# Mixture of experts with three choices per token: the inner layer's weights as a moving operand, read through a register, instead of loaded tile by tile

## The chip, the cores and the metric

One core of one Trainium2 chip runs the whole program. The metric is the device time of one execution in microseconds. The kernel is a decoder of four layers with twelve sublayers; the change is inside one of them, the feed-forward sublayer of the third layer (stage 8 in the code, `mixture_top3`). The median of three runs before is 2776.63 us (2773.84 to 2779.97).

## The reference, cut to what matters

There are 8 x 256 = 2048 tokens of 256 features. The sublayer computes, for each token, a shared expert and the three most probable of fifteen experts, each weighted with its softmax probability:

```
shared = relu(xt @ sW1 + sb1) @ sW2 + sb2
probs = softmax(xt @ router_W + router_b)
top_p, top_i = top_k(probs, 3)               # E = 15, cw holds top_p at top_i
h = relu(einsum('nd,edh->neh', xt, eW1) + eb1)   # eW1: 15 x 256 x 256
ye = einsum('neh,ehd->ned', h, eW2) + eb2        # eW2: 15 x 256 x 256
x = layernorm(x + shared + einsum('ned,ne->nd', ye, cw))
```

All of it is in 32-bit floating point.

## The kernel before, in words

Each sublayer is a block in which every engine has its own instruction list; engines meet at semaphores, and a barrier stands between blocks. The weights of a sublayer are one packed array that SP (SyncE) loads into `K.weights` while the sublayer before runs; so `W["w1"]` (32 tiles of 128 x 256, two for each expert and two for the shared one) and `W["w2"]` (the same) are both on chip when stage 8 starts.

The stage then has four parts.

1. Routing. TensorE (PE), VectorE (DVE) and ScalarE (ACT) compute the probabilities, the three choices, and for each (token, choice) a slot in a list that is sorted by expert and padded to whole tiles of 128 slots. There are `TILED` = 62 tiles, each belonging to one expert; `table` holds the expert of each tile. ACT copies the tokens into three sheets (L3014, L3017), one for each choice, 258 words a row: 256 features, the weight, and the place to which the result goes. In the kernel before sheet 0 lies on top of `W["w1"]` at the start of `K.weights`, sheet 1 above the weights, sheet 2 in the work area.
2. GpSimd (POOL) scatters the sheets into the HBM array `rows_in` with 48 indirect DMAs (L2881), while PE computes the shared expert.
3. The loop over the 62 tiles, which the change rewrites. For tile j:
   - SP loads the tile's 128 rows (129 KB, `load_rows`, L2814) into one of eight buffers `xt`; from the ninth on it waits until the scatter of the tile eight before has landed (L2813). It reads the tile's expert from `table` into a register (L2833), loads this expert's part of w1, 256 KB, from HBM into one of six places in `slots_w` (L2837), and its bias, 1 KB (L2839). At j = 8, 16, 24 and 32 it also issues a quarter of the next stage's weights, 960.5 KB (`load_next`, L2822). All of these are on SP's one queue, in this order.
   - PE turns the rows (`turn_row`, two 128 x 128 transposes, L2953), DVE copies them out of PSUM (L3119).
   - PE computes the hidden values already transposed (`hidden`): w1 is the stationary operand and the turned rows of 128 tokens are the moving one, four matmuls with 128 columns.
   - ACT applies bias and relu, one 128 x 128 half at a time, as the bias is one per partition (L3030).
   - PE multiplies with w2 (`outer`): here the hidden values are stationary and w2 is the moving operand, 256 columns, at an address that a PE register holds. PE reads eight experts at a time from `table` into registers (L2988).
   - DVE scales the result with the token's weight (L3126) and POOL scatters it to `rows_back` (L2888).

   The order on PE is written out by hand: in step j it does `turn_row(j)`, `hidden(j-1)`, `outer(j-2)`. DVE does `store_row(j)`, `store_out(j-2)`.
4. When all scatters have landed, SP loads the three results of each token (L2847), PE adds them, and the layer norm follows.

A 32-bit matmul shows as two MATMUL records (x8 for the four of `hidden`, x4 for the two of `outer`), a transpose as one.

Of the kernel before, what the change touches and what calls it, by code (L numbers as in the profile page):

```python
# [21 lines left out]
ACT = mybir.ActivationFunctionType  # L22
# [21 lines left out]
def allocate_signals(sem):  # L44
# [91 lines left out]
    S.k_rounded = sem("k_rounded")  # L136
    S.gate_stored = sem("gate_stored")
    S.zeros_done = sem("zeros_done")
    S.gate_done = sem("gate_done")
    return S, [S.x_copied, S.gate_done], 93  # L140

# [84 lines left out]
def weights_are_in(engine, K, stage):  # L226
    engine.wait_ge(K.weights_loaded, 16 * (K.stages.index(stage) + 1))
# [2533 lines left out]
def mixture_top3(nc, K):  # L2761
# [4 lines left out]
    RING, ROWS, SETS, REGS = 4, 8, 6, 8  # L2766

    above = words(8)
    sheets = [K.weights[:, 0:TILES * ROW], K.weights[:, above:above + TILES * ROW],
              A(TILES * ROW)]  # L2770
    sheets = [s.rearrange("p (i c) -> p i c", i=TILES) for s in sheets]
    got = [K.weights[:, n * 2 * TOP * D:(n + 1) * 2 * TOP * D] for n in range(4)]
    slots_w = [K.weights[:, TILES * ROW + r * KT * D:TILES * ROW + (r + 1) * KT * D].rearrange("p (k c) -> p k c", k=KT)
               for r in range(SETS)]
    bias1 = A(SETS, 2)
    xt, xT, hT, y = A(ROWS, ROW), A(2, KT, P), A(2, KT, P), A(RING, D)
    hid = A(2, GROUP)
    lT = xT.rearrange("p n k t -> p (n k t)")
    tail = tail_buffers2(A)

# [12 lines left out]
    most = hot.rearrange("p c i e -> p (c i e)")[:, 0:44 * E].rearrange("p (j e) -> p j e", e=E)  # L2793

    rows_in = K.rows_in.rearrange("(n p) c -> p n c", p=P)
    parts = K.packed[8][:, 0:32 * D].rearrange("p (e c) -> p e c", c=2 * D)
    biases = K.packed[8][:, 64 * D:64 * D + 32].rearrange("p (e m) -> p e m", m=2)
    flat = "p e c i -> p (e c i)"
    half = 2 * TILES * E
# [3 lines left out]
    with turn(nc, K) as block:  # L2803
        @block.sync
        def _(sp):
            weights_are_in(sp, K, 8)
            sp.dma_start(W["b2"][E:E + 1, 0, :], W["sb2"][E:E + 1, 0, :]).then_inc(K.bias_copied, 16)
            sp.wait_ge(S.table_done, 1)
            sp.wait_ge(K.scattered_in, 16 * TOP * TILES)
            sp.wait_ge(K.rows_cleared, 96)  # L2810
            def load_rows(j):
                if j >= ROWS:
                    sp.wait_ge(K.sent[(j - ROWS) % RING], 16 * ((j - ROWS) // RING + 1))  # L2813
                sp.dma_start(xt[:, j % ROWS, :], K.rows_in[j * P:(j + 1) * P, :]).then_inc(K.row_loaded[j % ROWS], 16)  # L2814

            def load_next(n):
                at, width = PLACE[9], words(9) // CHUNKS
                done = K.weights_part
                if n == CHUNKS - 1:
                    sp.wait_ge(K.weights_part, 16 * n)  # L2820
                    done = K.weights_loaded
                sp.dma_start(K.weights[:, at + n * width:at + (n + 1) * width],  # L2822
                             K.packed[9][:, n * width:(n + 1) * width]).then_inc(done, 16)

            with sp.register("expert") as expert:
                load_rows(0)
                load_rows(1)
                for j in range(TILED):
                    if j + 2 < TILED:
                        load_rows(j + 2)  # L2830
                    if j >= 8 and j % 8 == 0 and j // 8 <= CHUNKS:
                        load_next(j // 8 - 1)
                    sp.reg_load(expert, table[0:1, j:j + 1])  # L2833
                    e = sp.snap(expert, min_val=0, max_val=E - 1)
                    if j >= SETS:
                        sp.wait_ge(S.inner_stored, j - SETS + 1)
                    sp.dma_start(slots_w[j % SETS], parts[:, bass.ds(e, 1), :].rearrange("p e (k c) -> p (e k) c", k=KT)  # L2837
                                 ).then_inc(K.expert_loaded[j % SETS], 16)
                    sp.dma_start(bias1[:, j % SETS, :], biases[:, bass.ds(e, 1), :].rearrange("p e m -> p (e m)")  # L2839
                                 ).then_inc(K.expert_loaded[j % SETS], 16)  # L2840
            for r in range(RING):
                sp.wait_ge(K.sent[r], 16 * len(range(r, TILED, RING)))
            by_token = K.rows_back.rearrange("(b i p c) d -> b p i (c d)", b=B, i=2, p=P)
            for b in range(B):
                if b >= 4:
                    sp.wait_ge(S.back_summed, b - 3)
                sp.dma_start(got[b % 4].rearrange("p (i c) -> p i c", i=2), by_token[b]  # L2847
                             ).then_inc(K.back_loaded[b % 4], 16)

        @block.gpsimd  # L2850
        def _(p):
# [12 lines left out]
            nc.gpsimd.affine_select(out=before16, in_=before16, compare_op=ALU.is_gt, fill=0.0, base=0,  # L2864
                                    pattern=[[1, P]], channel_multiplier=-1)
            nc.gpsimd.memset(keep[:, :, 0, 0:1], 0.0).then_inc(S.pool_step, 1)
            weights_are_in(p, K, 8)
            for c in range(TOP):
                ins = nc.gpsimd.iota(sheets[c][:, :, D + 1:D + 2].rearrange("p i a -> p (i a)").bitcast(U32),
                                     pattern=[[TOP * P, TILES]], base=c, channel_multiplier=TOP)  # L2870
# [23 lines left out]
        def _(pe):  # L2894
# [53 lines left out]
            def turn_row(j):  # L2948
                pe.wait_ge(K.row_loaded[j % ROWS], 16 * (j // ROWS + 1))
                if j >= 2:  # L2950
                    pe.wait_ge(S.row_stored, j - 1)
                for k in range(KT):
                    ins = nc.tensor.transpose(K.bank[j % 2][:, k * P:(k + 1) * P], xt[:, j % ROWS, k * P:(k + 1) * P],  # L2953
                                              K.ident[:])
                ins.then_inc(S.row_turned, 1)

            def hidden(j):
                pe.wait_ge(K.expert_loaded[j % SETS], 32 * (j // SETS + 1))
                pe.wait_ge(S.row_stored, j + 1)
                if j >= 2:  # L2960
                    pe.wait_ge(S.inner_stored, j - 1)
                for m in range(2):
                    ins = mm(nc, K.bank[2 + j % 2][:, m * P:(m + 1) * P],
                             [(slots_w[j % SETS][:, k, m * P:(m + 1) * P], xT[:, j % 2, k, :]) for k in range(KT)])
                ins.then_inc(S.inner_done, 1)

            def outer(j, e):
                pe.wait_ge(S.inner_stored, j + 1)
# [6 lines left out]
            pe.wait_ge(S.y_added, B)  # L2975
            pe.wait_ge(S.shareT_stored, GROUPS)
            pe.wait_ge(S.table_done, 1)
            owners = [pe.alloc_register(f"owner{n}") for n in range(REGS)]
            of = {}
            for j in range(TILED + 2):  # L2980
                if j < TILED:
                    turn_row(j)
                if 1 <= j <= TILED:
                    hidden(j - 1)
                if 2 <= j:
                    if (j - 2) % REGS == 0:
                        n = min(REGS, TILED - (j - 2))
                        pe.reg_load(owners[0:n], table[0:1, j - 2:j - 2 + n])  # L2988
                        for i in range(n):
                            of[j - 2 + i] = pe.snap(owners[i], min_val=0, max_val=E - 1)  # L2990
                    outer(j - 2, of[j - 2])
            def sum_back(b):
                pe.wait_ge(K.back_loaded[b % 4], 16 * (b // 4 + 1))
                if b >= 4:
# [14 lines left out]

        @block.scalar  # L3010
        def _(a):
            weights_are_in(a, K, 8)
            for c in (2, 0):
                nc.scalar.copy(sheets[c][:, :, 0:D], K.x_tok[:]).then_inc(S.x_copied, 1)  # L3014
            a.wait_ge(S.max_done, 1)
# [9 lines left out]
            for j in range(TILED):  # L3025
                a.wait_ge(S.inner_done, j + 1)
                if j >= 2:
                    a.wait_ge(S.out_done, j - 1)
                for m in range(2):
                    ins = nc.scalar.activation(hT[:, j % 2, m, :], K.bank[2 + j % 2][:, m * P:(m + 1) * P], ACT.Relu,  # L3030
                                               bias=bias1[:, j % SETS, m:m + 1])
                ins.then_inc(S.inner_stored, 1)
            for b in range(B):
                batch_store(nc.scalar.copy, a, K, b, 6 + b % 2)

        @block.vector
        def _(v):
# [91 lines left out]
            for j in range(TILED + 2):  # L3129
                if j < TILED:  # L3130
                    store_row(j)
                if j >= 2:
                    store_out(j - 2)

            def add_back(b):
                x2 = K.x_tok[:, 2 * b:2 * b + 2, :]
# [1654 lines left out]
```

## Time and profile before

| | us |
|---|---|
| median of three runs | 2776.63 |
| the profiled execution's own time | 2774.84 |
| its span, first to last instruction | 2773.1 |
| stage 8, first instruction | 1289.8 |
| first and last turn of a row tile in the loop | 1387.45, 1542.86 |
| PE busy over the whole span | 2315.0 (83%) |

The profile is of one execution. Times within it are microseconds from the start of the span. The granted clock is given as a share of TensorE's full 2.4 GHz; a stretch at 0.5 is at 1.2 GHz. PE's busy time is a sum over overlapping records, so in the loop the start of one group and the start of the next say more than the length of either.

### The profile page before, as it was taken

What the parts mean: (1) busy time and instruction counts of PE and PEld (TensorE: products, weight loads), DVE (VectorE), ACT (ScalarE), POOL (GpSimd) and SP (SyncE); (2) the same over time, 40 slices, a digit from 0 to 9 for tenths busy, and PEclk for the clock granted to TensorE, in tenths of its full rate; (3) what the DMA queues carried; (4) which work ended last, traced back from release to release, by engine and by line L of the source; (5) the groups of instructions that cost most, each with busy time, mean ns of one, the idle gap of its engine ahead of it and who ended that gap; (6) DMA issues with size and microseconds to landing.
All of it is one profiled execution on the core that took longest, in us unless ns stands there. A gap on an engine that the chain in (4) does not pass through costs nothing. (4 is left out here: it accounts for less than half of the span.)

```text
span 2773.1 us, 39253 instructions
## 1 busy us (share of the span) xinstructions
PE 2315.0 (83%) x13092; PEld 1663.2 (60%) x13092; DVE 1422.1 (51%) x4229; ACT 1025.0 (37%) x2591; POOL 699.1 (25%) x656
## 2 busy tenths in 40 slices
PE   7985499878869839985788789698899798899898
PEld 5763377655547518864367566465466576466576
DVE  3555022256758765547123467544677443677454
ACT  3433111145525510035022156343565432565432
POOL 1102311110024343211633200263443100433111
PEclk9987699979969859997799899899999999999899
DMA  9032211173000010030287411400000000000000
GB/s 245 1 151 81 83 50 42 46 150 13 1 6 1 5 53 1 1 126 1 92 240 209 145 36 25 152 11 31 1 1 1 1 1 1 1 1 1 20 23 20
DMA packets 121173, 143.66 MB, mean 52 GB/s; under 512 B 47507, under 2 KB 101013, under 8 KB 119184
## 3 DMA queue, kind: packets, MB, share of 16 engines
q1 hardware_dynamic: 112240, 120.16, 15.5%
q0 software_dynamic: 8736, 20.99, 2.1%
q8 instruction: 109, 1.79, 0.3%
q14 instruction: 88, 0.72, 0.1%
HBM read 96.18 MB, written 47.90 MB: 52 GB/s over the span
## 5 line engine op out<-in xcount | busy, mean ns | idle before, releaser
L249 PE MATMUL bank<-work,weights 128*128 128x256 f32 (+3 forms) x2432 | 541.3, 380 | 42.2 <-DMA work<-in_weights 21.1
L249 PEld LDWEIGHTS bank<-work,weights 128*128 128x128 f32 (+1 forms) x2432 | 415.5, 193 | 138.2 <-DMA work<-in_weights 27.8
L249 PE MATMUL bank<-weights,work 128*128 128x256 f32 (+4 forms) x1520 | 412.6, 409 | 53.1 <-POOL work L2318 35.0
L249 PEld LDWEIGHTS bank<-weights,work 128*128 128x128 f32 (+1 forms) x1520 | 278.5, 196 | 152.7 <-issue 68.3
L633 POOL TENSOR_TENSOR work<-work,minus_half 128x2 f32<-128x2 f32 x96 | 69.7, 726 | 859.0 <-DVE work L626 859.0
L249 PE MATMUL bank<-weights,x_feat 128*128 128x512 f32 (+2 forms) x576 | 211.5, 500 | 25.5 <-PEq L211 14.6
L658 ACT COPY x_feat<-bank 128x512 f32<-128x512 f32 x80 | 46.7, 584 | 343.3 <-PE bank L650 342.9
L249 PEld LDWEIGHTS bank<-weights,x_feat 128*128 128x128 f32 x576 | 106.1, 196 | 84.2 <-issue 60.1
L249 PE MATMUL bank<-x_feat,weights 128*128 128x256 f32 (+3 forms) x400 | 120.4, 479 | 35.6 <-PEq L211 31.0
L4090 ACT ACTIVATE work<-work 128x128 f32<-128x128 f32 (+1 forms) x256 | 137.0, 543 | 1.5 <-DVE work L4162 1.5
L1523 DVE TENSOR_TENSOR work<-bank,work 128x384 f32<-128x384 f32 (+1 forms) x64 | 31.4, 491 | 189.6 <-ACT work L1441 189.6
L249 PEld LDWEIGHTS bank<-x_feat,weights 128*128 128x128 f32 (+1 forms) x400 | 79.5, 217 | 65.3 <-issue 51.7
L650 PE MATMUL bank<-ident,x_tok 128*128 128x128 f32 x320 | 61.2, 325 | 46.1 <-DVE x_tok L641 44.0
L249 PE MATMUL bank<-work 128*128 128x256 f32 (+3 forms) x326 | 72.9, 362 | 31.1 <-ACT work L2692 7.6
L3030 ACT ACTIVATE work<-bank,work 128x128 f32<-128x128 f32 x124 | 38.7, 363 | 141.9 <-PE bank L249 129.5
L4482 DVE SCALAR_TENSOR_TENSOR work<-bank,weights,work 128x256 f32<-128x256 f32 x96 | 45.5, 481 | 87.4 <-ACT work L4420 86.3
L3905 POOL TENSOR_TENSOR work<-work,minus_half 128x8 f32<-128x8 f32 x32 | 52.4, 1636 | 144.4 <-DVE work L4206 144.4
L1341 POOL DMA_INDIRECT rows_back<-work x40 | 38.8, 971 | 195.3 <-DVE work L1531 195.3
L2888 POOL DMA_INDIRECT rows_back<-work x62 | 60.2, 972 | 106.3 <-DVE work L3126 83.4
L4420 ACT ACTIVATE work<-bank,weights 128x256 f32<-128x256 f32 x80 | 37.9, 474 | 128.8 <-PE bank L249 128.7
L4154 DVE CUSTOM_DVE_ANT_0 work<-bank,work 128x128 f32<-128x128 f32 (+1 forms) x256 | 75.7, 352 | 16.9 <-PE bank L3953 16.9
L3126 DVE TENSOR_SCALAR work<-bank,work 128x256 f32<-128x256 f32 x62 | 30.0, 484 | 105.5 <-PE bank L249 75.8
(461 smaller groups left out, 4651.3 us busy)
## 6 DMA issues: line engine op xcount, KB each, us to landing
weights<-in_weights SPq DMA_DIRECT2D x62, 256.0 KB
weights<-in_weights SPq DMA_DIRECT2D x1, 12296.0 KB
weights<-in_weights SPq DMA_DIRECT2D x1, 9360.0 KB
weights<-in_weights SPq DMA_DIRECT2D x1, 8488.0 KB
work<-rows_in SPq DMA_DIRECT2D x62, 129.0 KB
rows_in<-ident SPq DMA_DIRECT2D x2, 3968.0 KB, 36.7
weights<-rows_back SPq DMA_DIRECT2D x8, 768.0 KB, 4.5
work<-rows_in SPq DMA_DIRECT2D x8, 645.0 KB, 4.2
```

The source lines that it names most:

```text
L249: ins = nc.tensor.matmul(out, lhsT, rhs, start=(i == 0), stop=(i == len(pairs) - 1))
L633: nc.gpsimd.tensor_tensor(t.rstd[:, n, :], t.rstd[:, n, :], K.minus_half[:, 0:2], ALU.pow).then_inc(K.S.rstd_done, 1)
L650: ins = nc.tensor.transpose(K.bank[bank][:, (2 * k + i) * P:(2 * k + i + 1) * P], K.x_tok[:, 2 * b + i, k * P:(k + 1) * P], K.ident[:])
L658: copy(K.x_feat[:, :, b * L:(b + 1) * L], K.bank[bank][:, :].rearrange("p (k t) -> p k t", k=KT)).then_inc(K.S.xT_stored, 1)
L1341: nc.gpsimd.indirect_dma_start(K.rows_back, bass.IndirectOffsetOnAxis(ap=to, axis=0), y[:, r, :], None, bounds_check=TOP * T - 1, oob_is_e ...
L2888: nc.gpsimd.indirect_dma_start(K.rows_back, bass.IndirectOffsetOnAxis(ap=to, axis=0), y[:, r, :], None, bounds_check=TOP * T - 1, oob_is_e ...
L3030: ins = nc.scalar.activation(hT[:, j % 2, m, :], K.bank[2 + j % 2][:, m * P:(m + 1) * P], ACT.Relu, bias=bias1[:, j % SETS, m:m + 1])
L3905: nc.gpsimd.tensor_tensor(rk, norm[:, 1, :], K.minus_half[:, 0:H], ALU.pow).then_inc(S.rk_done, 1)
L4090: ins = nc.scalar.activation(probs[:, u % 3, s, at:at + width], probs[:, u % 3, s, at:at + width], ACT.Exp, bias=bias[:, u % 2, i, s:s + 1 ...
L4154: ins = nc.vector.tensor_tensor_reduce(probs[:, u % 3, s, at:at + width], K.bank[SM[s]][:, at:at + width], seen[:, at:at + width], 1.0, -3 ...
L4420: nc.scalar.activation(gelu[:, n % 2, :], K.bank[n % RING][:, L:2 * L], ACT.Gelu, bias=W["b1"][:, layer, HT + f:HT + f + 1]).then_inc(S.ge ...
L4482: nc.vector.scalar_tensor_tensor(out=hid[rows, b % 2, f, :], in0=K.bank[n % RING][rows, 0:L], scalar=W["b1"][rows, layer, f:f + 1], in1=ge ...
```

## The change

- The load of each tile's part of w1 (L2837) and its six places go. `inner` takes w1 where it lies, as the moving operand at an address in a PE register, with the turned rows as the stationary operand: two matmuls with 256 columns in place of four with 128. Its result has the tokens in the partitions, so it must be turned: ACT copies it to `mid` (128 x 256), PE turns it with two transposes into bank 6 or 7 (`turn_mid`), and ACT applies bias and relu to that as before (`rectify`).
- The order on PE in step t becomes `turn_row(t)`, `inner(t-1)`, `turn_mid(t-2)`, `outer(t-3)`: one step more from the rows to the result. ACT does `store_mid(t-1)`, `rectify(t-2)`; DVE `store_row(t)`, `store_out(t-3)`. The eight experts are read into registers before `inner` instead of before `outer`, into two sets of registers in turn.
- Sheets 0 and 1 now both lie above the weights, so that w1 stays whole. POOL no longer waits for the weights, and ACT waits for them after the first two sheets instead of before.
- Two semaphores are added to the range that each barrier clears (93 to 95).

```
-    slots_w = [K.weights[:, TILES * ROW + r * KT * D:...]...]
+    mid = hid[:, 0, :].rearrange("p (n d) -> p n d", n=2)
...                                                        # SP
-                    sp.dma_start(slots_w[j % SETS], parts[:, bass.ds(e, 1), :]...).then_inc(K.expert_loaded[j % SETS], 16)
                     sp.dma_start(bias1[:, j % SETS, :], biases[:, bass.ds(e, 1), :]...).then_inc(K.expert_loaded[j % SETS], 16)
...                                                        # PE
-            def hidden(j):
-                pe.wait_ge(K.expert_loaded[j % SETS], 32 * (j // SETS + 1))
+            def inner(j, e):
                 pe.wait_ge(S.row_stored, j + 1)
+                if j >= 2:
+                    pe.wait_ge(S.mid_stored, j - 1)
+                mm(nc, K.bank[2 + j % 2][:, 0:D],
+                   [(xT[:, j % 2, k, :], W["w1"][:, bass.ds(2 * e + k, 1), :].rearrange("p o c -> p (o c)"))
+                    for k in range(KT)]).then_inc(S.inner_done, 1)
+            def turn_mid(j):
+                pe.wait_ge(S.mid_stored, j + 1)
                 if j >= 2:
                     pe.wait_ge(S.inner_stored, j - 1)
                 for m in range(2):
-                    ins = mm(nc, K.bank[2 + j % 2][:, m * P:(m + 1) * P],
-                             [(slots_w[j % SETS][:, k, m * P:(m + 1) * P], xT[:, j % 2, k, :]) for k in range(KT)])
-                ins.then_inc(S.inner_done, 1)
+                    ins = nc.tensor.transpose(K.bank[6 + j % 2][:, m * P:(m + 1) * P], mid[:, j % 2, m * P:(m + 1) * P], K.ident[:])
+                ins.then_inc(S.mid_turned, 1)
...
+            for t in range(TILED + 3):
+                if t < TILED:
+                    turn_row(t)
+                if t % REGS == 1 and t <= TILED:           # eight experts into owners[at:at + n]
+                    pe.reg_load(owners[at:at + n], table[0:1, t - 1:t - 1 + n])
+                if 1 <= t <= TILED:
+                    inner(t - 1, of[t - 1])
+                if 2 <= t <= TILED + 1:
+                    turn_mid(t - 2)
+                if 3 <= t:
+                    outer(t - 3, of[t - 3])
...                                                        # ACT
+            def store_mid(j):
                 a.wait_ge(S.inner_done, j + 1)
+                if j >= 2:
+                    a.wait_ge(S.mid_turned, j - 1)
+                nc.scalar.copy(mid[:, j % 2, :], K.bank[2 + j % 2][:, 0:D]).then_inc(S.mid_stored, 1)
+            def rectify(j):
+                a.wait_ge(S.mid_turned, j + 1)
+                a.wait_ge(K.expert_loaded[j % SETS], 16 * (j // SETS + 1))
```

## Rows read from the trace of the kernel before

**Rows 1.** Windows, the loop as one: length, busy time (instructions) of each engine, granted clock, DMA share, GB/s
```profile
1387.00:1548.00 161.00, 137.80 (x868) 120.35 (x868) 50.64 (x124) 38.73 (x124) 58.29 (x60) 0.94 0.75 216
```

**Rows 2.** Waits in the loop, 1387 to 1548: us in total, times, longest
```profile
PE bank L249 <- DMA work<-in_weights: 21.1, 15, 3.8
SPq L2814 <- DMA rows_back<-work: 20.8, 21, 2.7
```

**Rows 3.** Timeline of one undisturbed step: start, us, instructions [idle before]
```profile
1444.57 1.06 PE L249 MATMUL bank<-work,weights 128*128 128x128 f32 x8
1445.46 1.03 PE L249 MATMUL bank<-weights,work 128*128 x4
1445.66 0.62 ACT L3030 ACTIVATE work<-bank,work 128x128 f32<-128x128 f32 x2 [1.35 <-PE bank L249]
1446.33 0.38 PE L2953 MATMUL bank<-ident,work 128*128 128x128 f32 x2
1446.53 0.48 DVE L3126 TENSOR_SCALAR work<-bank,work 128x256 f32<-128x256 f32 x1 [1.16 <-issue]
1446.55 1.06 PE L249 MATMUL bank<-work,weights 128*128 128x128 f32 x8
1447.79 0.97 POOL L2888 DMA_INDIRECT rows_back<-work  x1 [1.01 <-issue]
```

**Rows 4.** Timeline at the loop's start and end
```profile
1385.28 1.29 SPq L2814 DMA_DIRECT2D work<-rows_in  x3
1387.45 1.09 PE L2953 MATMUL bank<-ident,work 128*128 128x128 f32 x4 [14.72 <-DMA work<-rows_in]
1390.19 2.07 PE L249 MATMUL bank<-work,weights 128*128 128x128 f32 x8 [1.65 <-DMA work<-in_weights]
1394.51 0.38 PE L2953 MATMUL bank<-ident,work 128*128 128x128 f32 x2
...
1542.86 0.38 PE L2953 MATMUL bank<-ident,work 128*128 128x128 f32 x2
1547.87 0.48 DVE L3126 TENSOR_SCALAR work<-bank,work 128x256 f32<-128x256 f32 x1 [0.60 <-PE bank L249]
```

**Rows 5.** Timeline around the first `load_next`, and after the third
```profile
1400.50 0.97 POOL L2888 DMA_INDIRECT rows_back<-work  x1 [1.00 <-issue]
1404.21 0.33 SPq L2814 DMA_DIRECT2D work<-rows_in  x1
1404.45 0.97 POOL L2888 DMA_INDIRECT rows_back<-work  x1 [1.01 <-issue]
1404.59 0.42 SPq L2822 DMA_DIRECT2D weights<-in_weights  x1
1410.47 0.33 SPq L2814 DMA_DIRECT2D work<-rows_in  x1
1411.14 1.16 PE L249 MATMUL bank<-work,weights 128*128 128x128 f32 x8 [2.76 <-DMA work<-in_weights]
...
1452.45 2.08 PE L249 MATMUL bank<-work,weights 128*128 128x128 f32 x8 [3.77 <-DMA work<-in_weights]
```

**Rows 6.** Sources: the 128 x 256 copy of ACT elsewhere, and PE's register loads (ns min/median/max)
```profile
L3368 ACT COPY work<-bank x16: 372/372/405, 1627.4 to 1767.3; 128x256 f32<-128x256 f32 x16
L2988 PEldq TENSOR_LOAD <-work x8: 588/602/1021, 1392.1 to 1536.4; - x8
```

**Rows 7.** Timeline of a step with a register load
```profile
1516.93 1.16 PE L249 MATMUL bank<-work,weights 128*128 128x128 f32 x8 [0.51 <-DMA work<-in_weights]
1518.46 1.13 PE L249 MATMUL bank<-weights,work 128*128 x4 [0.37 <-issue]
```

**Rows 8.** Stage 9, 1650 to 1700 as a window, and transposes among PE's groups, 1650 to 1750
```profile
1650.00:1700.00 50.00, 48.67 (x338) 34.07 (x337) 35.39 (x84) 31.76 (x113) 3.31 (x5) 1.00 0.12 24
L3267 PE MATMUL bank<-ident,work 128*128 128x128 f32 x163 | 21.9, 277 | 0.0
```

**Rows 9.** Timeline at the start of stage 8
```profile
1289.82 3.62 ACT L3014 COPY work<-x_tok 128x4096 f32<-128x4096 f32 x1 [1.24 <-PEq L211]
```

More of the change, by code:

```diff
@@ L138, in allocate_signals @@
     S.zeros_done = sem("zeros_done")
+    S.mid_stored = sem("mid_stored")
+    S.mid_turned = sem("mid_turned")
     S.gate_done = sem("gate_done")
-    return S, [S.x_copied, S.gate_done], 93
+    return S, [S.x_copied, S.gate_done], 95
 SPEC = {
@@ L2768, in mixture_top3 @@
     above = words(8)
-    sheets = [K.weights[:, 0:TILES * ROW], K.weights[:, above:above + TILES * ROW],
+    sheets = [K.weights[:, above:above + TILES * ROW], K.weights[:, above + TILES * ROW:above + 2 * TILES * ROW],
               A(TILES * ROW)]
@@ L2772, in mixture_top3 @@
     got = [K.weights[:, n * 2 * TOP * D:(n + 1) * 2 * TOP * D] for n in range(4)]
-    slots_w = [K.weights[:, TILES * ROW + r * KT * D:TILES * ROW + (r + 1) * KT * D].rearrange("p (k c) -> p k c", k=KT)
-               for r in range(SETS)]
     bias1 = A(SETS, 2)
@@ L2795, in mixture_top3 @@
     rows_in = K.rows_in.rearrange("(n p) c -> p n c", p=P)
-    parts = K.packed[8][:, 0:32 * D].rearrange("p (e c) -> p e c", c=2 * D)
     biases = K.packed[8][:, 64 * D:64 * D + 32].rearrange("p (e m) -> p e m", m=2)
@@ L2836, in _ @@
                         sp.wait_ge(S.inner_stored, j - SETS + 1)
-                    sp.dma_start(slots_w[j % SETS], parts[:, bass.ds(e, 1), :].rearrange("p e (k c) -> p (e k) c", k=KT)
-                                 ).then_inc(K.expert_loaded[j % SETS], 16)
                     sp.dma_start(bias1[:, j % SETS, :], biases[:, bass.ds(e, 1), :].rearrange("p e m -> p (e m)")
@@ L2866, in _ @@
             nc.gpsimd.memset(keep[:, :, 0, 0:1], 0.0).then_inc(S.pool_step, 1)
-            weights_are_in(p, K, 8)
             for c in range(TOP):
@@ L2962, in hidden @@
                 for m in range(2):
-                    ins = mm(nc, K.bank[2 + j % 2][:, m * P:(m + 1) * P],
-                             [(slots_w[j % SETS][:, k, m * P:(m + 1) * P], xT[:, j % 2, k, :]) for k in range(KT)])
-                ins.then_inc(S.inner_done, 1)
+                    ins = nc.tensor.transpose(K.bank[6 + j % 2][:, m * P:(m + 1) * P], mid[:, j % 2, m * P:(m + 1) * P],
+                                              K.ident[:])
+                ins.then_inc(S.mid_turned, 1)
             def outer(j, e):
@@ L2977, in _ @@
             pe.wait_ge(S.table_done, 1)
-            owners = [pe.alloc_register(f"owner{n}") for n in range(REGS)]
+            owners = [pe.alloc_register(f"owner{n}") for n in range(2 * REGS)]
             of = {}
[L2980 to L2991, printed above, removed]
+            for t in range(TILED + 3):
+                if t < TILED:
+                    turn_row(t)
+                if t % REGS == 1 and t <= TILED:
+                    n = min(REGS, TILED - (t - 1))
+                    at = (t - 1) // REGS % 2 * REGS
+                    pe.reg_load(owners[at:at + n], table[0:1, t - 1:t - 1 + n])
+                    for i in range(n):
+                        of[t - 1 + i] = pe.snap(owners[at + i], min_val=0, max_val=E - 1)
+                if 1 <= t <= TILED:
[4 more added lines that the diff above has]
+                    outer(t - 3, of[t - 3])
             def sum_back(b):
@@ L3011, in _ @@
         def _(a):
-            weights_are_in(a, K, 8)
             for c in (2, 0):
                 nc.scalar.copy(sheets[c][:, :, 0:D], K.x_tok[:]).then_inc(S.x_copied, 1)
+            weights_are_in(a, K, 8)
             a.wait_ge(S.max_done, 1)
@@ L3024, in _ @@
                                          bias=W["b1"][:, 0, 2 * E + m:2 * E + m + 1]).then_inc(S.hid_stored, 1)
-            for j in range(TILED):
+            def store_mid(j):
                 a.wait_ge(S.inner_done, j + 1)
+                if j >= 2:
[4 more added lines that the diff above has]
+                a.wait_ge(K.expert_loaded[j % SETS], 16 * (j // SETS + 1))
                 if j >= 2:
@@ L3029, in _ @@
                 for m in range(2):
-                    ins = nc.scalar.activation(hT[:, j % 2, m, :], K.bank[2 + j % 2][:, m * P:(m + 1) * P], ACT.Relu,
+                    ins = nc.scalar.activation(hT[:, j % 2, m, :], K.bank[6 + j % 2][:, m * P:(m + 1) * P], ACT.Relu,
                                                bias=bias1[:, j % SETS, m:m + 1])
                 ins.then_inc(S.inner_stored, 1)
+            for t in range(1, TILED + 2):
+                if t <= TILED:
+                    store_mid(t - 1)
+                if t >= 2:
+                    rectify(t - 2)
             for b in range(B):
@@ L3127, in store_out @@
                                         ALU.mult).then_inc(S.out_stored, 1)
[L3129 to L3133, printed above, removed]
+            for t in range(TILED + 3):
+                if t < TILED:
+                    store_row(t)
+                if t >= 3:
+                    store_out(t - 3)
             def add_back(b):
```

## The prediction

> **What bounds the kernel now.** I read the windows first, then the waits of the loop, then its timeline, then the start of the stage. The windows show the loop over the 62 row tiles as 161 us with PE busy for 138 of them, the DMA engines for three quarters of the time and a granted clock of 0.94 [rows 1]. The waits say what PE lacks: the expert's w1 from HBM, 15 times and 21.1 us in all, up to 3.8 us at once [rows 2]. In the timeline the turns of tile 0 start at 1387.45 and those of tile 61 at 1542.86 [rows 4]: 155.4 us for 61 steps, 2.55 a step. An undisturbed step is shorter [rows 3]: `hidden` 0.89 (1444.57 to 1445.46), `outer` 0.87 (to 1446.33), the two turns 0.22 (to 1446.55), 1.98 together, and PE is never idle in it. 61 x 1.98 is 120.8, so 34.6 us of the loop is not PE's own work at full clock. It is 21.1 of waits on w1 and, beyond that, half clock: 0.06 of 161 us of clock missing means 19 us at half clock, of which about half, 9.7, is lost. The rest, 4, is smaller gaps. The half clock is partly a child of the waits: after the idle 3.77 us at 1452.45 the eight matmuls of `hidden` take 2.08 instead of 1.06 [rows 5].
>
> Two things make w1 late. The four `load_next` transfers go ahead of it on SP's queue: after the first (1404.59) PE idles 2.76, after the third 3.77 [rows 5]; there are four of them. And between them it is a ring: SP issues the rows of tile j+8, and behind them w1 of tile j+6, only when the scatter of tile j has landed, and SP is seen waiting for that 21 times [rows 2].
>
> **The change, part by part.** The profiled execution took 2774.84, 1.8 below the median of the runs; I work on its trace and add the difference at the end.
>
> *PE's work in a step.* `hidden` (0.89) becomes `inner`, the same shape as `outer`: two matmuls of 256 columns, 0.87. Two more transposes cost 0.22. The step is 0.22 + 0.87 + 0.22 + 0.87 = 2.18, 0.20 more than now. Over 61 steps that is 12.2 us of loss.
>
> *The load of w1.* With it go all waits on it, and 62 x 256 KB, 16 MB of some 35. What is next on PE? Each of its waits reaches back to work of a step before. ACT had 0.62 of work in a step [rows 3] and gets a copy of 128 x 256 at 0.37 [rows 6], about 1.0 of 2.18; `rectify` ends some 1.2 before `outer` wants it, and the copy to `mid` 1.5 before `turn_mid` does. DVE (0.48 and a row copy) and POOL (0.97 a scatter) have as much to do as now.
>
> *The ring, one step deeper.* `outer` of tile j now ends four steps after `turn_row(j)`, not three. From PE's step end at 1446.33 DVE ends at 1447.01 and POOL starts the scatter at 1447.79 [rows 3], 1.5 later. From scatter to the release of SP I take 3.7 (1400.50 to 1404.21, [rows 5]; this includes SP's own delay), from the issue of rows to the first turn 2.2 (1385.28 to 1387.45, [rows 4]). That makes 7.4. The next turn in the same buffer has 4 x 2.18 = 8.7 of time. So the rows come 1.3 us early and PE sets the pace. The bias, issued behind the rows, is wanted only by `rectify`, more than two steps later than the rows.
>
> *The four `load_next`.* A scatter issued just before the first (1404.45) released SP only at 1410.47, 6.0 instead of 3.7 [rows 5]. 2.3 more, less 1.3 of slack, is 1.0 of idle for each, 4 in all, where now they cost some 13 and two falls of the clock. Bounds: nothing, when the lighter traffic lets them pass sooner; 3.4 each, 13.6, when the rows end up as late as w1 did. I take 1.0, nearest to the scatter's row, and no clock loss from it, since even after the idle 2.76 the eight matmuls take 1.16, the time at full clock [rows 5].
>
> *The start.* Tile 0 still turns at 1387.45, as that hangs on the rows. Now `hidden(0)` waits for w1 until 1390.19 and the turns of tile 3 start at 1394.51 [rows 4]. Without the wait `inner(0)` starts once DVE has copied tile 0, about 1388.65; at half clock its 1.73, turn and `inner(1)` of 0.44 + 1.73 and `turn_mid(0)` of 0.44 give tile 3 at 1393.0. Then 58 steps of 2.18 are 126.4, and with 4 for `load_next` and 0.5 for chance tile 61 turns at 1523.9.
>
> *The end.* Now the last result is at 1547.87 + 0.48, 5.5 after the turn of tile 61 [rows 4]. The new tail has the rest of step 61, then 0.87 + 0.22 + 0.87, then 0.22 + 0.87, then 0.87, about 0.35 for ACT before the last `outer` and 0.6 for DVE: 7.1. So the last result comes at 1531.0 instead of 1548.35: 17.4 us earlier. Behind it nothing changes: scatter, loads, sum and norm move forward as they are.
>
> *Register work.* The address of `inner` costs register instructions on PE's sequencer, and the load of eight registers takes 0.59 to 1.02 [rows 6]. I cost both at nothing: `outer` has the same addresses and streams at 0.87 with no gap. Exposed, a register load costs this: at 1516.93 `hidden` began after a wait and `outer` followed 1.53 later instead of 0.89, 0.64 lost [rows 7]. The upper bound is that in every step, 39 us; below nothing there is no reason to go. I take zero: in the undisturbed steps PE's stream has no gap, and after the change the waits that let PE's sequencer fall behind are gone.
>
> *The rest.* ACT's copies started right at the start of the stage (1289.82, idle only for the barrier), so the weights' wait cost nothing and moving it gains nothing [rows 9]; the same for POOL, whose first work stood before its own wait. The sheets are the same size in other places. Relu, copy and exponential follow one another in this stage with no table load of ACT. Two more semaphores in a range that one instruction clears: nothing, at most 0.1 a barrier.
>
> **Two rules weighed.** Four transposes now stand in a step, 0.44 of 2.18, a fifth of PE's time. In stage 9 there are 163 transposes of one line alone in 100 us, at 0.11 each 18 us of PE's stream, at a granted clock of 1.00 [rows 8]. The Trainium skill, page "TensorE: Matmul & The Clock Gate" (Part 4: PE-mode transpose), says that transposes do not count as a busy PE for the clock. By that rule the loop could fall to half clock; the trace shows the share that the change reaches without it.
>
> The rows of tile 0 took 2.2 with little traffic about [rows 4], and I use the same in the loop. The Trainium skill, page "DMA: Bandwidth & Descriptors" (Latency and other measured facts), holds that a lighter load on HBM lowers the fixed cost of a transfer. By it the slack of the ring would grow and `load_next` cost nothing, 4 us more gained; by the row, nothing.
>
> **Rivals.**
> - *`load_next` keeps its price.* The rows queue behind it as w1 did. For: rows and w1 share SP's queue. Against: the rows are issued two tiles ahead and w1 was not. 3.4 each instead of 1.0, and two half-clock stretches of 7 us, 7 lost: 16.6 less gain, 2776. A middle way, 2.5 each, gives 2765.
> - *No stall at all.* 4.5 more gained, 2755.
> - *PE's sequencer becomes the bound* (slower). `inner` needs a register address, one more semaphore wait and a dependence on ACT in each step; if it cannot run ahead, each step shows a gap before `inner`. For: the 0.64 of [rows 7]. Against: `outer` does it in every step unseen. It decides from 17.4 / 61 = 0.29 a step; at 0.5 a step, 30 us, the time is 2790.
> - *Half clock in the loop* (slower), if transposes do not count: 61 more steps of 2.18, 133 less 17: 2892.
> - *Later clock.* The stretches at half clock after the loop may shift by one or two of them: 5 us either way.
>
> **How the numbers follow.** The forecast is 2774.84 - 17.4 = 2757.4 by the profiled execution, 2759.2 against the median. Chances: forecast with `load_next` at 0 to 2 us each, 0.70; price kept wholly or mostly, 0.16; the sequencer, 0.07; half clock, 0.02; something that cancels to no change, 0.05. The range from 2750 (no stall, and a favourable clock) to 2769 (3 us for each `load_next`, or an unfavourable clock) leaves 0.2 out. A measurement of this kernel can tell 0.2%, 5.5 us, from no change: faster 0.87, within 0.05, slower 0.08.
>
> **What would show it.** In the profile after: no wait on `in_weights` on PE in the loop; steps of 2.18 with `inner` at 0.87 and four transposes of 0.11; the granted clock of the loop at 0.97 or more; the loop's turns spanning about 136 us; PE waiting about four times for `rows_in`, a microsecond each; DMA near 130 GB/s. Steps of 2.4 and more without a DMA wait would prove me wrong on the sequencer or ACT; waits of 3 us and more on `rows_in`, on the ring.

## The result, and the profile after

The changed kernel takes 2755.43 us (median of five runs, 2751.02 to 2756.06), the kernel before 2774.82 in the same five rounds (2769.97 to 2779.97): ratio 0.9925, 95% interval 0.9909 to 0.9941, which is a gain of 21 us, or between 16 and 25. Forecast were 2759.2 and a gain of 17.4. One execution of e7 (2799.47 us) and one of the kernel before beside e9 to e12 (2989.53) ran at a lower granted clock and are in no median or ratio below.

First the loop as a window (the length, busy time of PE, its weight loads, DVE, ACT, POOL, then granted clock, DMA share and GB/s), against [rows 1]:

```profile
1385.00:1525.00 140.00, 136.32 (x736) 115.66 (x737) 49.77 (x121) 55.40 (x184) 57.00 (x59) 0.98 0.47 132
```

Both windows stop just short of the last result, so the loop's length is read further down, from the first turn to the last result. The granted clock is 0.98 where it was 0.94, and the DMA traffic 132 GB/s where it was 216. ACT works 55 us where it worked 39, and is still far from full. The waits of the changed loop after its start (us in total, times, longest), against [rows 2]:

```profile
PE bank L2950 <- DMA work<-rows_in: 3.0, 3, 1.3
PEld bank L2967 <- issue: 0.2, 1, 0.2
```

PE waited 21.1 us for w1; now it waits 3.0 for rows, three times. After the loop's start PE waits nowhere in front of `inner`. The timeline of a step, against [rows 3] (L2950 is `turn_row`, L2967 `turn_mid`, L3036 the copy to `mid`, L3044 `rectify`; the first line of L251 is `inner`, the second `outer`):

```profile
1393.35 0.38 PE L2950 MATMUL bank<-ident,work 128*128 128x128 f32 x2
1393.57 1.03 PE L251 MATMUL bank<-weights,work 128*128 x4
1394.43 0.38 PE L2967 MATMUL bank<-ident,work 128*128 128x128 f32 x2
1394.63 0.37 ACT L3036 COPY work<-bank 128x256 f32<-128x256 f32 x1 [1.27 <-PE bank L251]
1394.65 1.03 PE L251 MATMUL bank<-weights,work 128*128 x4
1394.81 0.97 POOL L2885 DMA_INDIRECT rows_back<-work  x1 [13.43 <-DVE work L3146]
1394.90 0.63 ACT L3044 ACTIVATE work<-bank,work 128x128 f32<-128x128 f32 x2
1395.52 0.38 PE L2950 MATMUL bank<-ident,work 128*128 128x128 f32 x2
```

Read PE's lines by their starts: 0.22 + 0.86 + 0.22 + 0.87 = 2.17, and the next step begins without a gap. The ends of the loop, against [rows 4]:

```profile
1385.19 1.21 PE L2950 MATMUL bank<-ident,work 128*128 128x128 f32 x4 [14.51 <-DMA work<-rows_in]
1386.89 2.07 PE L251 MATMUL bank<-weights,work 128*128 x4 [0.49 <-DVE work L3139]
...
1520.72 0.38 PE L2950 MATMUL bank<-ident,work 128*128 128x128 f32 x2
...
1527.18 0.48 DVE L3146 TENSOR_SCALAR work<-bank,work 128x256 f32<-128x256 f32 x1 [0.55 <-PE bank L251]
```

From the first turn to the last result it is 142.5 us (1385.19 to 1527.66) where it was 160.9: 18.4 less. The whole span is 18.8 less. The remaining 0.4 is the sum of two larger differences: the loop starts 2.3 us earlier, and what follows it takes 1.9 longer. I put both down to chance, though the change also moved the sheets and two waits ahead of the loop. The start varies by itself: in the kernels below the first turn lies anywhere from 1382.5 to 1387.6, and in e11, whose work before the loop is that of the kernel before to the instruction, it lies at 1383.37 where the kernel before has 1387.45. I therefore compare the loops of the profiles by their own length, from the turn of tile 0 to that of tile 61, beside the ratios of the runs.

Around the first `load_next`, against [rows 5]:

```profile
1402.46 0.43 SPq L2822 DMA_DIRECT2D weights<-in_weights  x1
1403.48 0.97 POOL L2885 DMA_INDIRECT rows_back<-work  x1 [1.20 <-DVE work L3146]
1408.10 0.33 SPq L2814 DMA_DIRECT2D work<-rows_in  x1
1409.37 1.63 SPq L2814 DMA_DIRECT2D work<-rows_in  x1
1411.91 0.33 PE L2950 MATMUL bank<-ident,work 128*128 128x128 f32 x1 [1.06 <-DMA work<-rows_in]
```

The scatter that follows it starts at 1403.48; SP issues the rows that hang on it 4.6 later (1408.10), and PE turns them 3.8 after that, having idled 1.06. Away from a `load_next` these two stretches are 2.7 (the median of the 26 tiles that are not among the seven turned behind one) and 2.2 (the median from issue to landing). So both have grown, the release of SP by 1.9 and the load of the rows by 1.6. Behind the third `load_next` it is the load almost alone:

```profile
1440.45 0.33 SPq L2814 DMA_DIRECT2D work<-rows_in  x1
1445.34 0.44 PE L2950 MATMUL bank<-ident,work 128*128 128x128 f32 x2 [0.64 <-DMA work<-rows_in]
```

These rows were issued only 3.1 after their scatter (1437.33), and were there 4.9 after the issue.

### The profile page after: what moved, and what is told of

Its sections match the earlier page's. It is cut to its first block and busy times, and to the rows that moved or that the text cites. A ratio compares the mean times of both kernels' runs of the same rounds, so it can differ in the third digit from the quotient of the medians.

```text
span 2754.3 us, 39126 instructions
## 1 busy us (share of the span) xinstructions
PE 2315.5 (84%) x12968; PEld 1658.9 (60%) x12968; DVE 1422.7 (52%) x4229; ACT 1042.2 (38%) x2653; POOL 699.1 (25%) x656
## 5 line engine op out<-in xcount | busy, mean ns | idle before, releaser
L251 PE MATMUL bank<-weights,work 128*128 128x256 f32 (+5 forms) x1768 | 474.7, 404 | 53.1 <-POOL work L2320 35.0
L251 PE MATMUL bank<-work,weights 128*128 128x256 f32 (+3 forms) x1936 | 469.2, 403 | 19.9 <-DVE work L4492 10.0
L251 PEld LDWEIGHTS bank<-work,weights 128*128 128x128 f32 (+1 forms) x1936 | 351.3, 191 | 109.9 <-issue 13.9
L251 PEld LDWEIGHTS bank<-weights,work 128*128 128x128 f32 (+2 forms) x1768 | 319.8, 195 | 155.4 <-issue 68.2
L251 PE MATMUL bank<-weights,x_feat 128*128 128x512 f32 (+2 forms) x576 | 213.5, 504 | 25.2 <-PEq L213 14.3
L251 PEld LDWEIGHTS bank<-weights,x_feat 128*128 128x128 f32 x576 | 107.3, 199 | 84.3 <-issue 59.8
L251 PE MATMUL bank<-x_feat,weights 128*128 128x256 f32 (+3 forms) x400 | 120.2, 479 | 35.5 <-PEq L213 30.8
L251 PEld LDWEIGHTS bank<-x_feat,weights 128*128 128x128 f32 (+1 forms) x400 | 79.8, 218 | 65.2 <-issue 51.6
L251 PE MATMUL bank<-work 128*128 128x256 f32 (+3 forms) x326 | 73.7, 365 | 31.1 <-ACT work L2694 7.6
L1443 ACT ACTIVATE work<-bank 128x384 f32<-128x384 f32 (+1 forms) x64 | 27.9, 437 | 146.9 <-PE bank L251 146.9
L643 DVE TENSOR_SCALAR x_tok<-x_tok,work 128x256 f32<-128x256 f32 x192 | 77.6, 447 | 9.9 <-POOL work L635 9.9
```

The source lines that it names most:

```text
L643: ins = nc.vector.tensor_scalar(x, x, t.mv[:, b % 2, i, 0:1], t.rstd[:, b % 2, i:i + 1], ALU.subtract, ALU.mult)
```

## The experiments

All ratios are against the kernel before, run on the same chip. The chips differ from group to group, so two kernels of the table are compared by their ratios; by the intervals of these, a difference of less than some 6 us (8 to 10 where e9, e11 or e12 is one of the two) is not told from none. The loop is from the turn of tile 0 to that of tile 61 in one profiled execution. It says where time went: by it every kernel gains less on the kernel before than by the ratios, by 1 to 9 us, so it is safest to compare loops with each other.

| kernel | median us | ratio, 95% interval | loop us | undisturbed step |
|---|---|---|---|---|
| before | 2774.82 | | 155.4 | 1.98 |
| after | 2755.43 | 0.9925 (0.9909 to 0.9941) | 135.5 | 2.17 |
| e1_no_w1_load | 2748.02 | 0.9903 (0.9885 to 0.9920) | 132.5 | 1.98 |
| e2_w1_traffic_kept | 2767.00 | 0.9967 (0.9957 to 0.9977) | 151.8 | 2.17 |
| e3_fixed_addresses | 2753.34 | 0.9910 (0.9894 to 0.9926) | 132.9 | 2.17 |
| e4_turn_mid_twice | 2764.25 | 0.9951 (0.9933 to 0.9969) | 144.9 | 2.39 |
| e5_before_16_rows | 2747.00 | 0.9885 (0.9868 to 0.9901) | 132.9 | 1.98 |
| e6_after_16_rows | 2752.32 | 0.9906 (0.9889 to 0.9922) | 131.9 | 2.17 |
| e7_act_copies_w1 | 2738.63 | 0.9861 (0.9842 to 0.9881) | 122.8 | 1.98 |
| e8_act_copies_16_rows | 2738.21 | 0.9852 (0.9836 to 0.9869) | 121.3 | 1.98 |
| e9_after_17_chunks | 2750.46 | 0.9902 (0.9870 to 0.9934) | 131.8 | 2.17 |
| e10_w1_traffic_loose | 2769.06 | 0.9970 (0.9955 to 0.9984) | 148.5 | 2.17 |
| e11_before_next_weights_late | 2759.66 | 0.9932 (0.9908 to 0.9956) | 144.3 | 1.98 |
| e12_after_next_weights_late | 2751.28 | 0.9904 (0.9873 to 0.9934) | 131.8 | 2.17 |

**e1.** One part of the change alone: the load goes, nothing is added. It leaves out what the load brought, so its results are not those of the reference. PE's wait counts 16 instead of 32, for the bias alone.

```
-                    sp.dma_start(slots_w[j % SETS], parts[:, bass.ds(e, 1), :]...).then_inc(K.expert_loaded[j % SETS], 16)
```

> The kernel before without the load of each tile's w1 (the hidden values are computed from whatever lies in the six places; everything else, the bias load and the order on every engine included, is as before). My theory: what the change gains is the end of PE's waits for w1, and what it pays is 0.19 us of PE a step for the two transposes. Without the load and without the transposes the steps are 1.98; what is left is the ring, where the bias of tile j+6 arrives about 8.0 us after the step start it hangs on and is wanted after 8.1, and the four load_next at 2 to 3 us each. Loop from the turns of tile 0 to those of tile 61: 121 + 10 = 131 us, program about 24 us faster than before, that is 5 to 8 us faster than after. Rival (the waits come from SP's ring and not from w1): the waits move to the bias with nearly their old size, loop about 150, 5 us faster than before.

Measured: 27 us faster than before (22 to 32), with a loop of 132.5 where 131 was expected. The rival's 150 is far off, and my theory holds. Against after it is 6 us by the ratios, just within the noise, and 3.0 in the loop. PE's remaining waits, 7.0 us (5 times) where there were 21.1 (15), are on the bias, in the same semaphore.

**e2 and e10.** The opposite: the dependence goes, the traffic stays.

```
+                    sp.dma_start(slots_w[j % SETS], parts[:, bass.ds(e, 1), :]...).then_inc(K.expert_loaded[j % SETS], 16)
+                a.wait_ge(K.expert_loaded[j % SETS], 32 * (j // SETS + 1))     # e2, in rectify
+                     ....then_inc(K.w1_loose[j % SETS], 16)                    # e10: PE, ACT and DVE never wait for it
```

In e10 only SP waits for this load: before it loads into the same place again, six tiles later, and behind the loop.

> The changed kernel, with the 256 KB of each tile's w1 still loaded from HBM, into words that nobody reads; rectify waits for it together with the bias. My theory (the gain comes from PE no longer depending on that load, and PE sets the pace): steps stay 2.17, the load_next waits grow by 1 to 2 us each, program within 2 to 8 us of after, 12 to 17 us faster than before. Rival (the gain is the lighter traffic, 16 MB less on the 16 DMA engines): the rows come late in most steps, steps of 2.4 and more, program within 5 us of before.

> As e2_w1_traffic_kept, 256 KB of w1 a tile into words that nobody reads, but rectify does not wait for it; only the end of the loop does. It parts the two readings of e2: if its lost 11.6 us came from ACT waiting for w1, this is within 3 us of after; if they came from the traffic (rows late behind w1 and load_next on SP's queue), this is as slow as e2, 8 to 12 us slower than after. I expect the second, as the longest wait on PE in e2 was for rows.

Measured: e2 is 9 us faster than before (6 to 12), where I expected 12 to 17, and 12 slower than after, where I expected 2 to 8; nor is it within the rival's 5 us of before. e10, without ACT's wait for w1, is no faster than e2, so the loss comes from the traffic. The window of e10's loop, and PE's waits for rows from 1384 to 1522:

```profile
1384.00:1533.00 149.00, 136.50 (x714) 112.85 (x715) 49.31 (x119) 54.25 (x178) 55.53 (x57) 0.97 0.82 230
```

```profile
PE bank L2958 <- DMA work<-rows_in: 20.3, 4, 14.6
PEld bank L2958 <- DMA work<-rows_in: 9.1, 10, 3.0
```

Of the 20.3, 14.6 lie before the loop. 230 GB/s is about what the kernel before had (216). The undisturbed steps of e10 are 2.17; the time goes at tiles 9 and 10, 18 and 19, 26, and 32 to 34, thus behind each `load_next`, 13 us over 2.17 a step there (some 2 of them by a fall of the clock behind the second), and 3.5 in single steps of 2.4 to 3.2 elsewhere. So the change's gain has two parts. To take w1 off PE's path is worth 8 us (4 to 12), the price of the two transposes included; to take its traffic away is worth another 12, with eight row buffers. What this traffic costs the changed kernel with sixteen was not tried.

The trace of e10 also shows where the rows are late. Behind the first `load_next`:

```profile
1404.42 0.99 SPq L2816 DMA_DIRECT2D work<-rows_in  x1
1410.42 0.44 PE L2958 MATMUL bank<-ident,work 128*128 128x128 f32 x2 [1.68 <-DMA work<-rows_in]
```

These rows, of tile 11, were issued 4.0 after their scatter, hardly later than in this kernel's undisturbed steps (a median of 3.8), but PE had them only 6.0 after the issue. It is the same for tiles 19, 27 and 35 behind the other three: issued 3.6 to 4.3 after the scatter, turned 5.7 to 6.4 after the issue. So the time is lost after SP has issued them. ACT's four waits for the bias there, up to 2.9 us, each end 0.4 to 0.6 before the rows come and add nothing.

**e3.** No registers on PE: the first expert's weights for every tile.

```
-    W["w1"][:, bass.ds(2 * e + k, 1), :].rearrange("p o c -> p (o c)")
+    W["w1"][:, k, :]                                   # the same for w2; no reg_load
```

> The changed kernel with w1 and w2 of expert 0 for every tile, at fixed addresses: no register loads, no address arithmetic on PE. My theory: PE's sequencer runs ahead unseen, so 0 +- 2 us against after, steps of 2.17 as there. Rival (PE's sequencer adds to each step): steps shorter than 2.17 and 5 us or more faster than after.

Measured: 4 us faster than after by the ratios, which is within the noise, and the undisturbed step is 2.17 to the hundredth. The loop is 2.6 shorter, nearly all of it behind `load_next`, where two short waits (0.8 us) appear instead of three, and at the start. The sequencer as a bound is out. The one trace of it that I find: in after the step that follows each of the three waits takes 2.27, and e3 has no such step, so register work probably shows for 0.1 us there.

**e4.** The price of a transpose, and the clock.

```
-                for m in range(2):
+                for m in (0, 1, 0, 1):
```

> The changed kernel with the two transposes of turn_mid done twice, six transposes in a step instead of four, over a quarter of PE's stream. My theory: 0.22 us more a step, 13.4 us in all less 2 to 3 as the load_next waits are covered by the slower pace: 10 to 13 us slower than after, loop at full granted clock. Rival (transposes do not keep the clock up, as the Trainium skill's page TensorE: Matmul & The Clock Gate states): the granted clock falls in the loop, 60 us or more slower.

Measured: the loop is 9.4 longer than in after, and the program 7 us slower by the ratios (0 to 14), where I expected 10 to 13. 61 x 0.22 is 13.4, and the waits for rows with the steps behind them, 3.8 in after, are gone. The clock in its steady part, the same columns as above:

```profile
1390.00:1528.00 138.00, 138.00 (x810) 120.20 (x809) 46.69 (x115) 57.95 (x174) 55.53 (x57) 1.00 0.44 128
```

The granted clock is 1.00 with 0.66 us of transposes in a step of 2.39, 28% of PE's stream.

**e5 and e6.** Another cure for the ring: sixteen row buffers, in the words of the third sheet.

```
-    RING, ROWS, SETS, REGS = 4, 8, 6, 8
+    RING, ROWS, SETS, REGS = 4, 16, 6, 8
-    xt, xT, hT, y = A(ROWS, ROW), ...
+    xt = sheets[2]
```

> The kernel before with sixteen row buffers instead of eight (they lie in the words of the third sheet, which is scattered by then), so that a row load never waits for a recent scatter and SP can run ahead until the six places of w1 hold it. My theory (w1 was late because its issue hung on the scatter of eight tiles before, and on load_next ahead of it): SP runs six tiles ahead, the waits for w1 nearly end although all its traffic stays; steps of 1.98, loop 121 plus 3 to 8, program 22 to 30 us faster than before, faster than after. Rival (the 35 MB of traffic are too much for the DMA engines, and that is why after gains): the waits stay above 15 us, program at most 8 us faster than before.

> The changed kernel with sixteen row buffers. My theory: only the three waits for rows behind load_next go (3.0 us in its profile); 2 to 4 us faster than after. Rival: the rows are late for want of bandwidth during load_next, and no deeper ring helps; no difference.

Measured: e5 is 32 us faster than before (27 to 37; I expected 22 to 30), and 11 us faster than after by the ratios, with all of w1's traffic and no change on PE. The window of its loop:

```profile
1385.00:1518.00 133.00, 124.67 (x840) 113.51 (x841) 48.65 (x119) 37.48 (x120) 56.03 (x58) 0.95 0.88 261
```

and PE's waits for w1 in it:

```profile
PE bank L249 <- DMA work<-in_weights: 8.3, 5, 3.6
```

The engines carry 261 GB/s where they carried 216: they were not full before, w1 was asked for late. I had expected more of the loop, though: it is 132.9, where 121 plus 3 to 8 was forecast. Waits at its start and behind the first three `load_next` remain, and a fall of the clock behind the longest of them (3.6 us). e6 has no wait for rows once its loop has begun; that shortens the loop by 3.6 us, which the ratios (5 us) cannot tell from nothing.

**e9, e11, e12.** `load_next` by itself: in 17 parts, or behind the loop.

```
-    CHUNKS = 4                                         # e9
+    CHUNKS = 17
-                    if j >= 8 and j % 8 == 0 and j // 8 <= CHUNKS:     # e11, e12: moved behind the by_token loads
-                        load_next(j // 8 - 1)
```

> The changed kernel with the next stage's weights in 17 parts of 226 KB, one every three tiles, instead of 4 of 960.5 KB. My theory: a part of this size delays rows or scatter by less than the ring's slack of 1.3 us, so the three waits for rows (3.0 us) go: 1 to 4 us faster than after. Rival: 17 small waits in place of three, no gain.

> The kernel before with the next stage's weights loaded after the loop, behind the last load of results, in place of at tiles 8 to 32. My theory: its four waits of 2.8 to 3.8 us and the two falls of the clock behind them go, the small waits of the ring stay: 14 to 20 us faster than before. Rival (those waits are the ring's own, load_next only names them): under 8 us.

> The changed kernel with the same move. My theory: 3.0 us of waits go, steps of 2.17 throughout: 2 to 4 us faster than after. Rival: the next stage waits for its weights and loses as much or more.

Measured: e9 and e12 give the same loop, 131.8, that is 3.7 less than after and PE's pace throughout; the ratios give 6 us against after, with intervals of 9 either way, so it is the loops that show it. e11 is 19 us faster than before by the ratio (12 to 26), in the range, but its loop is only 11 shorter: waits for w1 of 12.4 us, 11 times, stay in it, and one of them brings a fall of the clock although no `load_next` is near:

```profile
1518.24 1.16 PE L249 MATMUL bank<-work,weights 128*128 128x128 f32 x8 [2.22 <-DMA work<-in_weights]
1519.24 1.86 PE L249 MATMUL bank<-weights,work 128*128 x4
```

The first group behind the idle 2.22 still takes its usual time, the next takes 1.86 instead of 1.03. In the kernel before, an idle 2.76 (at 1411.14) brought no such fall: how long PE idles does not decide it alone. The next stage's weights, moved behind the loop, cost the program nothing that shows.

**e7 and e8.** w1 on chip without a transpose. Before's order on PE; ACT copies the expert's words to a fixed place, at an address in its own register.

```
+            def copy_w1(j):                            # ACT; eight experts per reg_load
+                nc.scalar.copy(slots_w[j % 3], W["w1"][:, bass.ds(2 * of[j], 2), :]).then_inc(S.w1_copied, 1)
...                                                     # behind the relu of tile j: copy_w1(j + 2)
-                pe.wait_ge(K.expert_loaded[j % SETS], 32 * (j // SETS + 1))
+                pe.wait_ge(S.w1_copied, j + 1)         # hidden; e8 has sixteen row buffers as well
```

> w1 stays on chip as in the change, but ACT copies the expert's 128 x 512 words of each tile to one of three fixed places at an address in an ACT register; PE keeps the four matmuls with w1 stationary and the order of before, no transposes are added. My theory: PE's step is 1.98 again, ACT has 0.62 and about 0.55 of work in it and is hidden; the ring is one step shorter than in after; waits behind load_next 1 to 2.5 us each. Program 5 to 10 us faster than after, about as e1. Rival: ACT becomes late, because the copy of two tiles ahead stands before the relu of the next tile; steps of 2.2 and more, no better than after.

> The same with sixteen row buffers. My theory: steps of 1.98 without waits, loop 122 to 123 us, program 10 to 14 us faster than after, 30 to 34 us faster than before. Rival: ACT sets the pace, as in the rival of the run before.

Measured: e7 is 18 us (11 to 25) and e8 20 us (14 to 27) faster than after by the ratios, more than I expected; e8 is 41 us faster than before, the fastest kernel here, though not clear of e7. The loop of e8 is 121.3 where 61 x 1.98 is 120.8: of the 34.6 us that were not PE's own work 0.5 is left. One step of it; ACT's copy and relu fill 1.24 of 1.98:

```profile
1450.42 0.62 ACT L3036 COPY weights<-weights 128x512 f32 x1
1450.57 0.38 PE L2954 MATMUL bank<-ident,work 128*128 128x128 f32 x2
1450.79 1.06 PE L250 MATMUL bank<-work,weights 128*128 128x128 f32 x8
1451.68 1.03 PE L250 MATMUL bank<-weights,work 128*128 x4
1451.88 0.63 ACT L3046 ACTIVATE work<-bank,work 128x128 f32<-128x128 f32 x2 [0.85 <-PE bank L250]
1452.55 0.38 PE L2954 MATMUL bank<-ident,work 128*128 128x128 f32 x2
```

## Why the prediction was right, step by step

| step | forecast | measured |
|---|---|---|
| PE's step | 2.18 | 2.17 |
| waits for w1 on PE | none | none |
| waits behind `load_next` | four, 4 us | three, 3.0 us |
| slack of the ring, undisturbed | 1.3 | 2.3 |
| behind `load_next`, from scatter to the issue of rows | 6.0 | 4.6, 3.1, 4.6 |
| behind `load_next`, from the issue of rows to their turn | 2.2 | 3.8, 4.9, 4.0 |
| from the first turn to that of tile 3 | 5.5 | 6.0 |
| turns of tile 0 to 61 | 136.5 | 135.5 |
| from the last turn to the last result | 7.1 | 6.9 |
| register work, ACT's copy, DVE, POOL | hidden | hidden; e3: 2.17 without registers |
| granted clock, DMA in the loop | 0.97 or more, 130 GB/s | 0.98, 132 GB/s |

- *PE's work in a step* was read from the starts in [rows 3], and the shape of `outer` gave that of `inner` to the hundredth. Busy times would have misled: 1.06 and 1.03 stand for 0.89 and 0.87 of PE.
- *The ring, one step deeper*: the rows come early enough, and PE sets the pace except behind `load_next`. I took 3.7 from scatter to release of SP; in the changed kernel it is 2.7 when undisturbed (1401.32 to 1404.05, and the median of 26 tiles). So the slack is 2.3 and not 1.3.
- *The four `load_next`*: the 1.0 was right by luck. I had put the whole delay, 2.3 us, on the scatter, let the rows land in 2.2 as ever, and took off a slack of 1.3. In the trace the delay is 3.1 to 3.7 us behind the three that cost anything, about half of it or more in the load of the rows, which I had put at nothing; the slack is 2.3. Two terms, each some 1 us too small, cancel. The price is as low as it is because w1's traffic is gone, which I had named only in passing, in the bound of nothing. e10 shows the same order of work with that traffic at 13 us for the four. That was my first rival's price (13.6), which I had tied to the queue alone. Had the change kept the traffic, the loop would have taken 12 us more than forecast (148.5 for 136.5).
- *The start*: `inner(0)` began 1.70 after the first turn (1385.19 to 1386.89), where I had set 1.2; that is the 0.5 between 5.5 and 6.0.
- *What bounded the kernel before* I had right in kind: `load_next` and the ring. I gave `load_next` some 13 us and two falls of the clock, together about 20. In the trace of the kernel before, the six steps behind the four of them (5.00, 4.69, 7.73, 2.88, 7.54 and 2.99) are 19 us over 1.98 a step; the two stretches at half clock in them are 5.6 us long (as 1452.45 to 1458.04), not 7. Taking `load_next` away gives 19 (12 to 26) by the ratios of e11, and 11 by its loop, which has a fall of the clock of its own. The ring weighs at least as much: e5, which leaves `load_next` where it is, takes 22.6 off the loop and gains 32 (27 to 37). The two do not add up, probably because a wait behind `load_next` gives the ring time to catch up; that was not tried.
- *The rivals.* The sequencer: refuted by e3. Half clock by transposes: refuted at the shares tried, 20% (after) and 28% (e4) of PE's stream. `load_next` keeps its price: false here, true in e10 for the 13.6 (13 measured); but these 13 include the one fall of the clock that e10 has, where I had set two beside them. No stall at all: the loop would be 131.8, as e9 and e12 show, 3.7 us away.
- The rule of the Trainium skill that a lighter load on HBM lowers a transfer's fixed cost ("DMA: Bandwidth & Descriptors", Latency and other measured facts): the traces go its way, by about 1 us. From scatter to the issue of rows, SP's own delay included, the median of the undisturbed tiles is 3.7 before and 2.7 after, and 3.8 in e10, which is after with the traffic put back. But it did not make `load_next` free: the slack did grow, and the rows behind `load_next` came later than I had allowed for.

What stays open is why rows that SP has issued behind a `load_next` land late: because they stand behind its 960.5 KB in the same DMA queue, or because they share the engines with it and with w1. The two were not tried apart.

## What to carry to other kernels

When an engine waits for a load, look first at what the issue of that load waits for. Here it was the scatter of eight tiles ago, for which a row load ahead of it on the same queue waits; twice the row buffers (e5) gave more than the removal of 16 MB of traffic together with two transposes a tile. Count a pipelined engine's work by the starts of its groups, and the pace of a ring of buffers by its whole round (result, scatter, release, load) over the number of steps in it; compare the two. When a forecast comes out right, check its terms one by one against the trace: here a delay and a slack were both some 1 us too small, and only their difference was right. If an operand must be at a fixed address, a copy by an idle engine (ACT, 0.62 us a tile) is cheaper than to turn the product on the busy one (0.22 of PE's time, 61 times).

## What was not expected of the hardware

- A row load takes 0.33 us of SP's time to issue, but 1.63 and 1.71 at two places in the changed kernel's loop and up to 1.76 before. This happens behind a `load_next` and also far from one (in the kernel before at 1516.21, 1.37 for a bias of 1 KB). What SP waits for then the trace does not show.
- ACT reads at an address in a register at about the pace of a fixed one: 128 x 512 words in 0.61 to 0.62 us from SBUF to SBUF, 62 times without an exception in e8. Copies of that shape out of PSUM at fixed addresses take 0.58 to 0.60 in the same trace.
- Full clock was granted with 28% of PE's stream in transposes (e4, 1.00 over 138 us). By the rule of the Trainium skill weighed in the prediction ("TensorE: Matmul & The Clock Gate", Part 4: PE-mode transpose), transposes do not count as a busy PE for the clock; mixed with matmuls as here they did no harm, and a stream of transposes alone was not tried.
- Behind a `load_next` of 960.5 KB a row load of 129 KB, which lands in 2.2 us otherwise, took 3.8 to 4.9 us in the changed kernel and 5.7 to 6.4 in e10, counted from its issue by SP.
